# Recurrence of a one-layer decoder: GpSimd's scatter of tokens, its input copy and VectorE's normalising step change places

## The reference, cut to what matters

```python
x = x + attn(layernorm(x))                     # 16 query heads of 8, one key/value head
# recurrence over t, for all 128 sequences
xin = concat([layernorm(x)_t, a])
h0, c0 = lstm_cell(xin, h0, c0)                # 128 wide
h1, c1 = lstm_cell(h0, h1, c1)
q = h1 @ Wq.T
attn = softmax(einsum('bh,bsh->bs', q, context))
mixed = einsum('bs,bsh->bh', attn, context)
a = tanh(concat([mixed, h1]) @ Wo.T + bo)      # the output of step t
x = x + a
# feed-forward, top 1 of 8 experts, 128 -> 512 -> 128
gate = max softmax(layernorm(x) @ router_W + router_b)
x = x + gate * (relu(layernorm(x) @ W1[e] + b1[e]) @ W2[e] + b2[e])
```

## Time and profile before

| | |
|---|---|
| Median of 3 runs | 1565.74 us (1564.3 to 1566.23) |
| Profiled execution | 1570.4 us, span 1568.7 us |
| TensorE matmul / weight load busy | 1335.8 us (85%) / 1195.8 us (76%) |
| VectorE / ScalarE / GpSimd busy | 1089.8 us (69%) / 742.8 us (47%) / 599.5 us (38%) |
| The scatters of tokens on GpSimd | 64, 70.1 us in all, 1096 ns each |
| The copies of the next input on GpSimd | 389 to 420 ns each |

### The profile page before, as it was taken

The page is one execution under the profiler, slowest core; times in us unless marked ns, Lnnn a source line. Parts: engine busy times, 40 slices in busy tenths (PEclk is TensorE's granted clock), DMA queues, the critical chain, the costliest instruction groups (busy, mean ns, idle before and its releaser), DMA issues. The chain is left out here.

```text
span 1568.7 us, 83724 instructions
## 1 busy us (share of the span) xinstructions
PE 1335.8 (85%) x34523; PEld 1195.8 (76%) x34523; DVE 1089.8 (69%) x4580; ACT 742.8 (47%) x2203; POOL 599.5 (38%) x1485
## 2 busy tenths in 40 slices
PE   0867888888499999999999999999999999839997
PEld 0556666666388888888888888888888888729996
DVE  7778999999456666666666666666666666636664
ACT  0656777787234444444444444444444444315553
POOL 1337555555402333333333333333333333224444
PEclk9979999999699999999999999999999999959999
DMA  8000000000320000000000000000000000022332
GB/s 255 1 2 16 17 17 17 17 17 17 110 53 11 19 16 18 19 16 18 19 16 18 19 16 18 19 16 18 19 16 18 19 16 18 14 82 80 95 96 56
DMA packets 49055, 52.62 MB, mean 34 GB/s; under 512 B 6026, under 2 KB 42252, under 8 KB 48168
## 3 DMA queue, kind: packets, MB, share of 16 engines
q1 hardware_dynamic: 41040, 32.50, 7.4%
q0 software_dynamic: 5344, 12.66, 2.3%
q10 hardware_dynamic: 2296, 2.14, 0.4%
HBM read 28.31 MB, written 19.42 MB: 30 GB/s over the span
## 5 line engine op out<-in xcount | busy, mean ns | idle before, releaser
L1076 PE MATMUL sc_ab<-h_a,KH 128*128 128x48 f16 (+2 forms) x4096 | 123.2, 183 | 2.2 <-DVE h_a L1413 2.2
L1076 PE MATMUL sc_ab<-h_b,KH 128*128 128x48 f16 (+2 forms) x4096 | 123.4, 183 | 0.3 <-issue 0.2
L1149 ACT ACTIVATE gt_a<-z_a,sc 128x256 f32<-128x256 f32 x128 | 60.6, 474 | 128.9 <-PE z_a L1003 128.9
L1126 PEld LDWEIGHTS mx_ab<-pmv_b,VH 128*128 128x128 f16 x4096 | 107.1, 96 | 16.3 <-DVE pmv_b L1456 16.3
L1126 PE MATMUL mx_ab<-pmv_b,VH 128*128 128x16 f16 x4096 | 113.0, 169 | 5.3 <-DVE pmv_b L1456 0.4
L1003 PE MATMUL z_a<-h_a,WL 128*128 128x64 f16 x2304 | 112.4, 193 | 5.6 <-DVE h_a L1405 2.0
L1003 PE MATMUL z_b<-h_b,WL 128*128 128x64 f16 x2304 | 112.0, 193 | 5.6 <-DVE h_b L1405 0.4
L1076 PEld LDWEIGHTS sc_ab<-h_a,KH 128*128 128x128 f16 x4096 | 113.1, 96 | 2.3 <-DVE h_a L1413 2.3
L1076 PEld LDWEIGHTS sc_ab<-h_b,KH 128*128 128x128 f16 x4096 | 113.3, 96 | 0.7 <-issue 0.5
L1126 PE MATMUL mx_ab<-pmv_a,VH 128*128 128x16 f16 x4096 | 112.2, 169 | 0.4 <-DVE pmv_a L1456 0.2
L1149 ACT ACTIVATE gt_b<-z_b,sc 128x256 f32<-128x256 f32 x128 | 60.6, 473 | 107.0 <-PE z_b L1003 107.0
(11 more groups left out here) (295 smaller groups left out, 3847.9 us busy)
## 6 DMA issues: line engine op xcount, KB each, us to landing
xr<-sorted_x SPq DMA_DIRECT2D x71, 129.0 KB
X<-in_x SPq DMA_DIRECT2D x8, 512.0 KB, 8.2
XT<-in_ctxT SPq DMA_DIRECT2D x4, 1024.0 KB
x_scratch<-X SPq DMA_DIRECT2D x8, 512.0 KB, 3.2
x1r<-x_scratch SPq DMA_DIRECT2D x64, 64.0 KB, 1.9
X<-in_w SPq DMA_DIRECT2D x1, 2048.0 KB, 9.0
sorted_x<-zt SPq DMA_DIRECT2D x12, 129.0 KB, 3.7
out<-ys,xr POOLq DMA_INDIRECT x71
```

The lines of the kernel that those rows point to most:

```text
L1076: mm = nc.tensor.matmul(A.S[:, WIDE * n:WIDE * n + streamed(n)], KH[:, k, pair * P:(pair + 1) * P], A.h[1][:, 2 * n:2 * n + streamed(n) // ...
L1126: mm = nc.tensor.matmul(A.M[:, WIDE * n:WIDE * (n + 1)], VH[:, k, pair, :], A.pm[:, 2 * n:2 * n + WIDE // 2, :].rearrange("p b k -> p (b k)"),
L1149: nc.scalar.activation(L.gt[l][:, :, :].rearrange("p g b -> p (g b)"), L.z[l][:, 0:4 * GB], ACT.Tanh, scale=sc[:, I0 + l:I0 + l + 1]).then ...
```

## The change

GpSimd's scatter moves behind the copy of xs_a, and waits there until TensorE has turned the probabilities of group b in this half (`s_pt`). VectorE's `normalise` moves from the start of the even half to behind `cell(1)`, ahead of `hidden(1)`. Nothing else differs.

```diff
 # GpSimd, half()
                         if odd == 1 and live(t - 4):
                             if not isinstance(t, int) or t < T:
                                 place(t - 4, (m - 4) % SLOTS)
-                            scatter(t - 4, (m - 4) % SLOTS)
                         if L:
                             if not (isinstance(lt, int) and lt == T - 1):
 
                                 ready(L.s_ah, 2 * lt)
                                 pool.wait_ge(L.s_xu, lt + 1)
                                 pool.tensor_copy(L.xs[:, :, :], XTn(L, lt + 1)).then_inc(L.s_xs, 1)
+                        if odd == 1 and live(t - 4):
+                            if A:
+                                pool.wait_ge(A.s_pt, at + 1)
+                            scatter(t - 4, (m - 4) % SLOTS)
                         if odd == 0 and live(t - 2):
                             copy_xn(t - 2, (m - 2) % SLOTS)
 # VectorE, half()
                         if odd == 0:
-                            if live(t - 2):
-                                normalise(t - 2, (m - 2) % SLOTS)
                             if live(t - 4):
                                 gate(t - 4, (m - 4) % SLOTS)
...
                         if L:
                             cell(1)
+                        if odd == 0 and live(t - 2):
+                            normalise(t - 2, (m - 2) % SLOTS)
                         if odd == 1 and live(t - 3):
                             choose_first(t - 3)
```

## The result

The changed kernel takes 1556.12 us (median of 10 runs, 1554.3 to 1562.24), the kernel before beside it 1567.04 us (10 runs, 1564.3 to 1570.85): ratio 0.9936, 95% interval 0.9921 to 0.9951. The change is faster by 0.6%, 10 us, where 39 us were forecast; 1556 lies outside the range of 1510 to 1548. The profiled execution took 1556.52 us (span 1554.3), against 1570.4.

What follows compares the result with a forecast made beforehand. TensorE was taken to bound the recurrence, idling for sm_b while the scatter held the scores' release. Terms -52.2 + 12.0 + 1 = -39 us took the profiled 1570.4 to 1531, as a median 1526 us; range 1510 to 1548.

Steps and rivals of the forecast that it cites:

- (2): Scatter's new place, beside the value matmuls and h_a: holds nothing there, 0 us; ends 0 and 0.87 us a step.
- rival 3: The hold moves to the end of the value matmuls, making a_b 0.87 us late: 1579 us; chance 0.07.
- three terms of 0.1 us a step: Range's upper end: 0.3 us instead of 0.2 for (3), 0.1 for h_a, 0.1 for (4).
- (1): Odd half: sm_b no longer held after the scores by the scatter, 0.87 us in each of 60 steps: -52.2 us.
- (3): Even half: GpSimd's later copy of xs_b meets VectorE's second u_b, delaying h_b 0.2 us a step: +12.0 us.
- rival 1: Even half: the copy of xs_b slips clear of the u_b pair, costing nothing: 1514.5 us; chance 0.22.
- (4): XN (normalise) moved behind c_b: h_b not late, GpSimd's place later but nothing late, 0 us; otherwise 0.1 us a step.
- (5): End of the recurrence: rstd and the last LayerNorm come later behind the scatter, +1 us (0 to 1.6).
- Rival 2: At the new place the scatter locks out VectorE's h_a, 0.5 us a step, 30 us: 1556 us; chance 0.11.

Runs made afterwards that it cites:

- b1: The kernel before, unchanged, run again with its profile in group 4: 1566.91 us.
- c1: The kernel before, unchanged, run again with its profile in group 5: 1520.88 us.
- c2: The changed kernel, unchanged, run again in group 5: 1527.16 us, ratio 1.0038 to the kernel before.
- b2: The changed kernel, unchanged, run again in group 4: 1556.88 us, ratio 0.9927 to the kernel before.
- e2: The changed kernel with the scatter waiting for h_a of cell 1 instead of the turn, 1.6 us later in the step: 1544.43 us.
- e1: The changed kernel without the scatter on GpSimd; SyncE writes the tokens to fixed rows, sorting left out: 1520.13 us.
- e7: The changed kernel with a plain DMA from GpSimd's queue to fixed rows in place of the indirect scatter, sorting left out: 1520.65 us.
- e8: e1 with a memset of 1200 columns (1.10 us) on GpSimd in the scatter's place: 1520.32 us.
- b3: e1 plus an indirect scatter of 32 rows instead of 128, to an unread tensor, at the changed kernel's place; group 4: 1555.33 us.
- e5: The changed kernel with the scatter waiting for the scores of b instead of the turn of the probabilities: 1519.95 us.
- b4: The changed kernel without the scatter's wait for the turn, so right behind the copy of xs_a; group 4: 1524.87 us.
- e4: The kernel before with normalise moved behind cell(1) and nothing else: 1548.49 us, ratio 0.9875.
- e6: The changed kernel with two more unused matmuls of 256 columns ahead of TensorE's wait for pmv_b in the odd half: 1545.41 us.
- e3: The changed kernel with normalise back in its old place at the start of the even half: 1570.84 us.

## Why the prediction was wrong, step by step

The ledger in medians of runs, taken from groups 4 and 5 and so from two chips: 1566.9 (b1); without the hold 1520.9 (c1), -46.0; with the copy's meeting 1527.2 (c2), +6.3; with the stop and the falls 1556.9 (b2), +29.7. My sum had -52.2, +12.0, +1 and, for the last, 0.

**(2) is the step that failed: "I take 0".** I had read the hold as something that delays what TensorE releases, and asked only which releases fall into the first 1.37 us of the scatter. The value matmuls' end did not, by 0.07 us. But TensorE itself stops, from 0.9 to 1.3 us, and every matmul behind is late. The kernel before can't show whether it stops there as well: by 0.9 us TensorE has started the last of its gates' matmuls, and then it idles for sm_b. Its ends were 0 and 0.87 a step; the row tells 0.42, half-way, and that end of the range was given to rival 3 alone, at 0.07. With both ends held open for the sum, 0 to 52 us, the range would have held the time. (The range's upper end of 1548 is also some 4 us more than its three terms of 0.1 us a step give: 1526 + 18 = 1544.)

That the stop is the indirect DMA's is shown: it moves with it (e2), is gone without it (e1), with a plain DMA (e7) or a memset (e8) in its place, and is as long with a quarter of the rows (b3). It is not enough that the instruction is there: in e5, b4 and e4, in groups with the effect, TensorE starts three or more matmuls 0.95 to 1.25 us into the scatter in 57 of 57, 57 of 57 and 53 of 55 steps. In these TensorE pauses for h_a or sm_b within the scatter's first 0.9 us, and where it is stopped it had run without a pause; that this decides was not tested. The Trainium skill (SBUF — State Buffer, "Who interferes with whom") has it that TensorE and ScalarE never wait on anyone, since only VectorE shares a port with GpSimd. By that rule, my 0 was right; the hole of 0.42 us in 64 matmuls decides against it for this instruction.

**The falls of the clock** (13 us in the profile, 11 us by e6) were in no step and no rival. They are shown to hang on what TensorE does around the stop: the same stop later in the step (e2), or with two more matmuls ahead of it (e6), has none. The stop isn't needed for a fall (b4 has three). What decides in which steps the clock falls stays open: 11 of 59 in this profile, 13 in b2, 8 in b3.

**(1) was right in kind**, and somewhat large: sm_b follows the scores after 0.45 us and TensorE's wait for it is gone. But 52.2 came from one undisturbed step of 13.87 us; all steps together are 13.94 (c1), and the hold is worth 46.0.

**(3) was right in kind and hit only in part.** In c2 the copy starts 3.74 us behind the scatter's start (I had 3.77) and an u_b of 0.44 us stands beside it, as forecast, but it is the first of the pair, and the cost is 0.12 us a step, 7 us, not 0.2. Where the stop is present it costs 0, since the stop shifts u_b by 0.42 us past the copy but not GpSimd: rival 1's case, brought about by the stop. So the two costs don't add up: 25 us of stop less 7 of this, plus 11 to 13 for the clock, are the 29.7. The same page of the Trainium skill ("Summary: rules for kernel authors") says that a VectorE instruction with two inputs in SBUF contends with a GpSimd instruction that reads SBUF, and that the second one to issue fully blocks until the first finishes. That it contends, the trace shows; a full block would have ended u_b 0.22 us after the copy, and it ended 0.09 after it (899.99 to 899.90), as in the earlier trace rows.

**(4) was right in the sum** (h_b is not late), and XN's old place would have blocked VectorE, as written: e3 shows 15 us for it. What I missed is that this move, by itself, delays the scatter by 0.25 us in the kernel before and brings 20 us (e4). "Nothing is late" answered the wrong question, since late was what helped. **(5)** can't be told from the scatter of the runs.

**Rival 2** fell: h_a took 0.24 us beside the scatter. **Rival 3** had the right place and the wrong means. That my 1526 lies 1 us from c2 is luck: two terms were too large by 6 us each, with opposite signs, and in c2's group the kernel before has no hold to lose.

The best order found is e5's, one semaphore away from the change: 1519.95 us and 0.9706 (0.969 to 0.9723) of the kernel before, where the change has 0.9936 (0.9921 to 0.9951). It is the time of a kernel without the scatter.

## What to carry to other kernels

When a wait is removed by moving an instruction, the cost moves with it; ask what it does to every engine at the new place, and bound that by the whole loss seen at the old one, not by the model that explained it. The cheap place for the scatter was one where TensorE's stream has pauses and nobody waits for what it releases (e5, b4): there the same instruction cost nothing that can be measured (e5) or 4 us (b4). And a gain that consists of dodging an interference is worth what the interference is: time the kernel before in every group, for here the same change is 0.7% faster or 0.4% slower, depending on the group.

## What the hardware showed that I had not expected

- An indirect DMA issued by GpSimd (1.09 us for 128 rows, 0.97 for 32) stops TensorE's stream from about 0.9 to 1.3 us after its start, where that stream ran without a pause before. It also holds TensorE's releases, whether the stream stops or not: one due at 0.45 us reached VectorE only at 1.37 us (the kernel before), one due at 0.20 us at 0.57 us (e4), one due at 0.75 us was recorded at 1.33 us (e5). Why a release is held before the stop begins stays open.
- The effect as a whole came and went by groups of runs: present in the first comparison and in groups 1, 2 and 4, absent in groups 3 and 5 (46 us of the same kernel, where the runs of one group lie within 9 us). The chips' numbers in the results were 3, 15 and 6 with it, 3 and 9 without, so it isn't told by the number; what sets it is open, and no run here could choose it.
- A stop of 0.42 us in TensorE's stream was followed, in 11 of 59 steps, by a fall of the granted clock to its lower level for some 3 us, at 1.2 us a step. Two more matmuls ahead of it prevented all of them.
